# Layer 1's norms in one operation per tile, with weights and shifts moved behind the turn

## What is computed

```python
def layer0(q_feat, kv_feat, ...):
    qn  = layer_norm(q_feat,  g_q,  be_q)     # (x - mu) * rsqrt(var + 1e-5) * gamma + beta
    kvn = layer_norm(kv_feat, g_kv, be_kv)
    q = einsum('bnq,eq->bne', qn,  Wq) + bq
    k = einsum('bmk,ek->bme', kvn, Wk) + bk
    v = einsum('bmk,ek->bme', kvn, Wv) + bv
    attn = softmax(einsum('bne,bme->bnm', q, k))
    return q_feat + einsum('bne,fe->bnf', attn @ v, Wd) + bd

def layer1(x, ctx, mask, ...):                # 8 heads of 256
    Q, K, V = x @ Wq, ctx @ Wk, ctx @ Wv
    attn = softmax(where(mask, Q K^T / 16, -inf))
    return layer_norm((attn @ V) @ Wo + x, gamma, beta)
x = layer0(x, ctx_768, ...)
return layer1(x, ctx_768, mask, ...)
```

## Time and profile before

| | before |
|---|---|
| median of 3 runs | 502.14 us (501.59 to 502.42) |
| the profiled execution: its time | 503.23 us |
| its span, first to last instruction | 501.4 us |
| mean granted TensorE clock | 0.995 |
| TensorE busy in the span | 473.7 us |
| VectorE, ScalarE, POOL busy | 332.4, 290.8, 244.6 us |

### The profile page before, as it was taken

The page is one execution under the profiler, slowest core; times in us unless marked ns, Lnnn a source line. Parts: engine busy times, 40 slices in busy tenths (PEclk is TensorE's granted clock), DMA queues, the critical chain, the costliest instruction groups (busy, mean ns, idle before and its releaser), DMA issues.

```text
span 501.4 us, 7564 instructions
## 1 busy us (share of the span) xinstructions
PE 473.7 (94%) x2424; PEld 395.0 (79%) x2424; DVE 332.4 (66%) x681; ACT 290.8 (58%) x480; POOL 244.6 (49%) x151
## 2 busy tenths in 40 slices
PE   0999999999999999999999999999999999999993
PEld 0777787777878888888888888888888888778893
DVE  4999866476685658565856585667657665664566
ACT  3657477468665656565656565666556564646331
POOL 4636763555855363627172727363635453353003
PEclk9999999999999999999999999999999999999998
DMA  8413004667865656565647474747484746661002
GB/s 261 147 44 126 1 25 123 210 203 231 251 201 187 209 169 209 169 210 167 221 156 230 147 225 156 250 136 254 142 256 135 244 149 190 171 205 43 1 1 84
DMA packets 53974, 81.97 MB, mean 163 GB/s; under 512 B 5792, under 2 KB 43072, under 8 KB 53824
## 3 DMA queue, kind: packets, MB, share of 16 engines
q1 hardware_dynamic: 44992, 50.16, 34.5%
q10 hardware_dynamic: 8960, 31.54, 16.8%
HBM read 49.16 MB, written 32.51 MB: 163 GB/s over the span
## 4 chain that ended last, share of the span: by engine, by line
PE 79%; DVE 8%; ACT 4%; issue 3%; DMA 3%; POOL 2%; SPq 1%; DVEq 0%; POOLq 0%; ACTq 0%
PE ps_scores L621 29%; PE ps_o L645 6%; PE ps_o L653 6%; PE ps_o L646 6%; PE ps_o L652 6%; PE ps_o L647 6%; PE ps_task L569 3%; PE ps_task L568 3%; PE ps_task L567 3%; DMA ctx_raw<-in_context 2%; PE ps_out L567 2%; PE ps_out L568 1%; PE ps_out L569 1%; PE ps_turn L637 1%; PE ps_out L739 1%
## 5 line engine op out<-in xcount | busy, mean ns | idle before, releaser
L514 POOL TENSOR_TENSOR probs_t_lo<-probs_t_lo,probs_t_hi 128x1024 fp32r<-128x1024 f32 (+1 forms) x75 | 146.7, 1968 | 177.2 <-ACT probs_t_hi L1013 177.2
L1013 ACT ACTIVATE probs_t_hi<-probs_t_lo 128x1024 fp32r<-128x1024 f32 (+1 forms) x75 | 64.6, 881 | 38.4 <-DMA probs_t_lo<-scratch 37.9
L621 PE MATMUL ps_scores<-key_hi,q_hi 128*128 128x512 f32 x144 | 57.7, 401 | 1.3 <-DVE neg_scores L1346 0.8
L1333 DVE RECIPROCAL row_inv<-row_sum 128x1 f32<-128x1 f32 x72 | 11.2, 158 | 71.9 <-PE ps_scores L621 70.1
L645 PE MATMUL ps_o<-probs_t_hi,val_hi 128*128 128x512 f32 (+1 forms) x144 | 56.7, 394 | 1.5 <-issue 0.9
L621 PE MATMUL ps_scores<-key_rem,q_lo 128*128 128x512 f32 x144 | 56.6, 393 | 0.5 <-DVE q_lo L1428 0.3
L621 PE MATMUL ps_scores<-key_rem,q_hi 128*128 128x512 f32 x144 | 56.6, 393 | 0.0
L621 PE MATMUL ps_scores<-key_lo,q_hi 128*128 128x512 f32 x144 | 56.6, 393 | 0.0
L621 PE MATMUL ps_scores<-key_hi,q_lo 128*128 128x512 f32 x144 | 56.4, 392 | 0.0
L646 PE MATMUL ps_o<-probs_t_lo,val_hi 128*128 128x512 f32 (+1 forms) x144 | 56.4, 391 | 0.0
L653 PE MATMUL ps_o<-probs_t_lo,val_rem 128*128 128x512 f32 (+1 forms) x144 | 56.3, 392 | 0.0
(11 more groups left out here) (254 smaller groups left out, 1094.4 us busy)
## 6 DMA issues: line engine op xcount, KB each, us to landing
probs_t_lo<-scratch SPq DMA_DIRECT2D x240, 128.0 KB, 3.0
...
```

The source lines that it names most:

```text
L514: nc.gpsimd.tensor_tensor(pt_lo[b][:, t, k, :], pt_lo[b][:, t, k, :].bitcast(f32), moved_part(j, k).bitcast(f32), ALU.subtract).then_inc(m ...
L621: last = pe.matmul(ps_scores[:, n], left, right[:, n], start=(i == 0), stop=(i == len(passes) - 1))
L1013: act.activation(moved_part(j, k), pt_lo[b][:, t, k, :].bitcast(f32), ACT.Copy)\
```

## The change

A layer-0 norm becomes one operation per tile: (x - mean) / sigma. ScalarE does it for x and for half of the context as scale and bias, with the bias (-mean/sigma) made by a new small VectorE operation (`shift_means`, which needs POOL's result); VectorE does it for the other context half with a two-scalar operation (`norm_context`). Gamma is applied later, where the turned chunks leave PSUM: features then lie on partitions, and gamma is a column, given as scale to ScalarE's rounding and to VectorE's subtraction; likewise when B leaves PSUM. The columns come from four 2-row transposes of the norm rows on PE (`gains`). The betas go into biases: VectorE reduces the weights against a broadcast beta row (`fold_bias`), PE adds products with `neg_be` to the query bias (T_VEC). The score shift is made on PE: w = two-part bias product (4 products), the constant (4), and 16 narrow products of the turned x with w in two parts (`turn_shift`), once for each batch. `sum_shift` and POOL's `bias_tiles` go. The context of batch 0 is loaded in two halves, `q_rows` is not broadcast any more, one kv row of 192 values is, behind the first weights; the norm rows come in three small DMAs ahead of the identity on ScalarE's queue. Roundings and waits change places as shown.

```diff
             sp.dma_start(resid[:, 0:QT, :], x_tiles[:, 0:QT, :]).then_inc(x_loaded[0], 16)
-            sp.dma_start(q_rows[:, :, :], rows_q.partition_broadcast(P)).then_inc(q_rows_loaded, 16)
-            sp.dma_start(ctx_raw[:, 0:KT, :], ctx_tiles[:, 0:KT, :]).then_inc(ctx_loaded[0], 16)
-            sp.dma_start(kv_rows[:, :, :], rows_kv.partition_broadcast(P)).then_inc(kv_rows_loaded, 16)
+            sp.dma_start(ctx_raw[:, 0:CTX_HALF, :], ctx_tiles[:, 0:CTX_HALF, :]).then_inc(ctx_loaded[0], 16)
+            sp.dma_start(ctx_raw[:, CTX_HALF:KT, :], ctx_tiles[:, CTX_HALF:KT, :]).then_inc(ctx_loaded[1], 16)
             sp.dma_start(ring[0][:, :], weights_a[0]).then_inc(ring_loaded[0], 16)
+            sp.dma_start(kv_row[:, :], rows_kv[1].partition_broadcast(P)).then_inc(kv_row_loaded, 16)
...
-            def bias_tiles(b, tiles, scaled_before, done):
...
-                done = b * (QT + CTX_HALF)
-                rsqrt(b, KT, LN_TILES, 2 * b + 1)
-                pool.wait_ge(q_rows_loaded, 16)
-                bias_tiles(b, range(KT, LN_TILES), done, x_normed)
+                rsqrt(b, KT, LN_TILES, 3 * b + 1)
...
-                rsqrt(b, 0, KT, 2 * b + 2)
-                pool.wait_ge(kv_rows_loaded, 16)
-                bias_tiles(b, range(CTX_HALF, KT), done + QT, ctx_normed[1])
+                rsqrt(b, 0, CTX_HALF, 3 * b + 2)
+                rsqrt(b, CTX_HALF, KT, 3 * b + 3)
...
-            pool.wait_ge(centred, LN_TILES + QT)
+            pool.wait_ge(x_normed, 2 * QT)
...
+            def turn_shift(b, bank):
+                for t in range(QT):
+                    q = slice(b * QUERIES + t * P, b * QUERIES + (t + 1) * P)
+                    for k in range(DT):
+                        pe.matmul(bank[:, 2 * t:2 * t + 2], xt_hi[:, k, q], w_pair[:, k, :], start=(k == 0), stop=False)
+                        last = pe.matmul(bank[:, 2 * t:2 * t + 2], xt_lo[:, k, q], w_pair[:, k, :],
+                                         start=False, stop=(k == DT - 1))
+                last.then_inc(shift_turned, 1)
...
-            pe.wait_ge(spread_made, DT)
-            pe.wait_ge(ring_loaded[0], 16)
-            raw = ring[0]
-            for k in range(DT):
...
             pe.wait_ge(ident_loaded, 16)
+            pe.wait_ge(norm_rows_loaded, 48)
+            for n in range(N_GAINS):
...
+            last.then_inc(gains_turned, 1)
             for c in range(X_CHUNKS):
                 turn_chunk(0, c)
             pe.wait_ge(piece_split, PC_A0 + 1)
             absorb(T_A0, 0)
             absorb(T_A0b, 1)
-            for n in range(3):
...
             for c in range(X_CHUNKS, CHUNKS):
                 turn_chunk(0, c)
+            pe.wait_ge(bias_folded, 1)
             pe.wait_ge(chunk_split, X_CHUNKS)
-            pe.wait_ge(task_free, T_VEC + 1)
+            raw = ring[0]
+            for d in range(DT):
+                for k in range(DT):
+                    last = pe.matmul(w_bank[:, d:d + 1], raw[:, k * DIM + d * P:k * DIM + (d + 1) * P],
+                                     bias_cols[:, k:k + 1], start=(k == 0), stop=(k == DT - 1))
+            last.then_inc(w_made, 1)
+            pe.wait_ge(task_free, T_A0b + 1)
+            pe.wait_ge(gains_made, 1)
+            for n in range(2):
...
+            last.then_inc(task_done, 1)
+            pe.wait_ge(chunk_split, X_CHUNKS)
             queries(T_Q0, 0, 0)
             queries(T_Q0b, 0, 1)
+            pe.wait_ge(w_split, 1)
+            for n in range(2 * DT):
+                last = pe.matmul(w_bank[:, DT:DT + 1], ones[:, :], shift_parts[:, n:n + 1],
+                                 start=(n == 0), stop=(n == 2 * DT - 1))
+            turn_shift(0, w_bank[:, V_SHIFT:V_SHIFT + 2 * QT])
             pe.wait_ge(chunk_split, CHUNKS)
...
+                if c == 0:
+                    pe.wait_ge(task_free, T_Q1 + 1)
+                    turn_shift(1, ps_task[:, 0:2 * QT])
...
+            act.dma_start(norm_rows[:, 0:DIM], rows_q).then_inc(norm_rows_loaded, 16)
+            act.dma_start(norm_rows[:, DIM:DIM + CTX], rows_kv).then_inc(norm_rows_loaded, 16)
+            act.dma_start(norm_rows[:, DIM + CTX:2 * DIM], rows_kv[:, P:CTX]).then_inc(norm_rows_loaded, 16)
+            act.dma_start(ident[:, :], identity).then_inc(ident_loaded, 16)
             act.dma_start(cols[:, :], vectors).then_inc(cols_loaded, 16)
-            act.dma_start(ident[:, :], identity).then_inc(ident_loaded, 16)
...
-            def scale_tiles(b, tiles, rstds):
...
+            def norm_tokens(b):
+                act.wait_ge(means_made, 2 * b + 1)
+                for t in range(KT, LN_TILES):
+                    n, x_tile = b * LN_TILES + t, b * QT + t - KT
+                    act.activation(xn[:, x_tile, :], resid[:, x_tile, :], ACT.Identity,
+                                   scale=rstd[:, n:n + 1], bias=neg_means[:, n:n + 1]).then_inc(x_normed, 1)
+            def norm_context(b):
+                act.wait_ge(means_made, 2 * b + 2)
...
-            act.wait_ge(cols_loaded, 16)
-            for n in range(2 * DT):
-                act.activation(spread[:, n, :], ones[:, :], ACT.Copy, scale=cols[:, C_BK + n:C_BK + n + 1])\
-                    .then_inc(spread_made, 1)
-            scale_tiles(0, range(KT, LN_TILES), 1)
+            act.activation(row_sum[:, 0:1], ones[:, 0:1], ACT.Copy)
+            norm_tokens(0)
             round_weights(16, 0)
+            act.wait_ge(gains_made, 1)
             for c in range(X_CHUNKS):
                 round_chunk(0, c)
-            scale_tiles(0, range(CTX_HALF, KT), 2)
+            norm_context(0)
+            double_context(0, 0)
             round_a(T_A0, 0, -1.0)
             round_a(T_A0b, 1, -1.0)
-            double_context(0, 0)
-            round_chunk(0, 2)
             double_context(0, 1)
-            for c in range(3, CHUNKS):
+            for c in range(2, CHUNKS):
                 round_chunk(0, c)
-            round_weights(16, 1)
             act.wait_ge(vec_made, 1)
             round_queries(T_Q0, 0, 0, 0)
             round_queries(T_Q0b, 0, 1, 0)
+            round_weights(16, 1)
+            act.wait_ge(bias_folded, 2)
+            for n in range(DT, 2 * DT):
+                act.activation(spread[:, n, :], ones[:, :], ACT.Copy, scale=bias_cols[:, n:n + 1]).then_inc(spread_made, 1)
             exp(-1, 0)
             round_b(T_B0, 0)
             round_b(T_B0b, 1)
             round_probs(-1, 0)
             exp(-1, 1)
-            scale_tiles(1, range(KT, LN_TILES), 3)
+            norm_tokens(1)
             round_weights(32, 0)
             round_probs(-1, 1)
             exp(-1, 2)
...
-            def ln_centre(b, tiles):
...
+            def norm_context(b):
+                dve.wait_ge(rstd_made, 3 * b + 2)
+                for t in range(CTX_HALF):
                     n = b * LN_TILES + t
...
+                    dve.tensor_scalar(kvn[b][:, t, 0:CTX], ctx_raw[:, b * KT + t, :], moments[:, n, 0:1],
+                                      rstd[:, n:n + 1], ALU.subtract, ALU.mult).then_inc(ctx_normed[0], 1)
+            def shift_means(b, first, end, rstds):
+                n = slice(b * LN_TILES + first, b * LN_TILES + end)
+                dve.wait_ge(rstd_made, 3 * b + rstds)
+                dve.scalar_tensor_tensor(neg_means[:, n], moments[:, n, 0], -1.0, rstd[:, n], ALU.mult, ALU.mult)\
+                    .then_inc(means_made, 1)
+            def fold_bias(side, raw, loaded):
+                dve.wait_ge(loaded, 16)
+                for k in range(DT):
+                    n = side * DT + k
+                    first = (DT + k if side == 0 else k) * DIM
+                    dve.tensor_tensor_reduce(
+                        out=probs[:, n * CTX:(n + 1) * CTX], in0=raw[:, first:first + CTX], in1=kv_row[:, :], scale=1.0,
+                        scalar=0.0, op0=ALU.mult, op1=ALU.add, accum_out=bias_parts[:, n:n + 1]).then_inc(bias_summed, 1)
...
+                dve.tensor_tensor(bias_cols[:, n], bias_parts[:, n],
+                                  cols[:, C_BK + side * DT:C_BK + (side + 1) * DT], ALU.add).then_inc(bias_folded, 1)
+            def split_w():
...
+                dve.tensor_tensor(w_pair[:, :, 1], made, w_pair[:, :, 0].bitcast(f32), ALU.subtract).then_inc(w_split, 1)
...
-            def sum_shift(b, tiles):
...
+            def finish_shift(b, bank):
...
-            dve.wait_ge(q_rows_loaded, 16)
-            ln_centre(0, x_token_tiles)
-            ln_stats(0, range(KT), ctx_loaded[0])
-            ln_moments(0, 0, KT)
+            ln_stats(0, range(CTX_HALF), ctx_loaded[0])
+            ln_moments(0, 0, CTX_HALF)
+            shift_means(0, KT, LN_TILES, 1)
+            ln_stats(0, range(CTX_HALF, KT), ctx_loaded[1])
+            ln_moments(0, CTX_HALF, KT)
+            dve.wait_ge(gains_turned, 1)
+            dve.tensor_copy(gains[:, :], vec_bank[:, V_GAINS:V_GAINS + 2 * N_GAINS])
...
             dve.wait_ge(piece_hi, HI_OF[PC_A0])
```

(33 more changed lines are left out.)

169 lines of the change are left out of this document (86 added, 83 removed).

## The result

The changed kernel took 510.84 us (median of four executions, 509.51 to 513.83) against 501.88 us for the kernel before (501.59 to 502.42) beside it: ratio 1.0189, interval 1.017 to 1.0208. The sign of the forecast was right; the size, +2.95 us, was a third of the 8.96 us measured, and the time lies outside the range. The profiled execution took 513.83 us, the longest of the four, its span 512.0.

What follows compares the result with a forecast made beforehand. TensorE, busy 94% of the span, was taken as the bound. Front +0.55, power wait +1.2 and batch 1's shifts +1.2 gave +2.95: profiled 503.23 becomes 506.2, and the median, 1.1 lower, 505.1 us (slower); range 501.2 to 507.0.

Steps and rivals of the forecast that it cites:

- The price of the narrow products: Front, before queries and scores: a one-column f32 product costs 0.12 us; w 4, query biases 12, constant 4 products.
- The clock: TensorE's front: no clock fall was forecast; products were priced at full-clock spacings, such as 0.235 us per query product.
- +0.55 forecast: Front, up to the end of the first scores: 0.55 us later than before, between -1.5 and +1.9.
- Rival C: Front: TensorE's slow start covers the weights' product, 2.9 instead of 1.45 us; with late loads +2.3, 506.9 us; chance 0.14.
- The loads: Front: 459 kB less ahead of the weights, landing at 9.9 to 10.8 instead of 12.0 us; first context half at 7.0.
- The cover for the identity: Front: the identity, moved to fourth on ScalarE's queue and wanted at about 10 us, is hidden by the x norm.
- The shifts: 16 narrow fp32r products at 0.12 us, 1.9 us in the front and among batch 0's values; net there +1.2.
- rival A: Front and values: narrow fp32r products cost 0.06 us each, 0.95 less in both places; +1.05, 503.2 us; chance 0.15.
- The power wait: Between minimum 0 and 1: VectorE's shift_means waits 1.1 us for POOL's power, plus 0.1 for the operation; +1.2 us.
- Rival D: Between minimum 0 and 1: VectorE's wait for POOL's power hides, 1.2 us less, 503.9 us; chance 0.13.
- Hidden work: VectorE before the first minimum: second fold (0.85 us) and small operations end 0.7 us before the scores, costing nothing.
- After 62 us: Rest of the kernel: assumed only to repeat what it did, shifted, its stream keeping its length; no cost.

Runs made afterwards that it cites:

- b1_narrow: Kernel before plus 14 narrow f32 products (28 instructions, results thrown away) in one piece behind its own: 509.98 us, ratio 1.013.
- b2_mixed: Kernel before plus 28 narrow instructions, scattered one or two products at a time between the wide query products: 507.14 us, ratio 1.0087.
- f1: Changed kernel with batch 1's first shift_means moved from ahead of the b splits to behind minimum 1: 510.22 us, ratio 1.0153.
- f3: Changed kernel plus six wide f32 products (results thrown away) on TensorE as soon as x is loaded: 511.68 us, ratio 1.0194.
- f4: Changed kernel with the wide query products ahead of the w and vector products, nothing left out: 510.49 us, ratio 1.0156.
- b3_noshift: Kernel before with the score shift left out and replaced by zero: 501.93 us, ratio 0.9987.
- h1_noshift: Changed kernel with the score shift left out (no w, constant or shift products on TensorE): 504.95 us, ratio 1.0047.
- h2_lean: h1_noshift with the norm's shift folded into the query bias on VectorE, remaining vector products between queries, power subtraction behind minimum 1: 503.63 us, ratio 1.0023.

## Why the prediction was wrong, step by step

*The price of the narrow products: the step that failed first.* The text read "0.95/8" as the price of a product. It is the price of an instruction, and a plain f32 product is two; the row's x8 were four products. So w, the vector and the constant were 8, 24 and 8 instructions where 4, 12 and 4 were priced. From the fold to the first query the sum had 2.0 us; 32 instructions at 0.115 are 3.7. With the constant the miscount is 2.1 us.

*The clock: not in the sum, nor in any rival.* The sum priced every product at the 2.4 GHz level, without a reason given, and this is the largest part of the error. From 21.1 us, inside the vector, the changed kernel's front runs at 1.2 GHz. Worked out from its rows against full speed: 20 narrow instructions at 0.21 instead of 0.115 are 1.9 us, twelve query products (25.25 to 30.51) 5.25 instead of 2.85, the constant 0.3, and in the second fall, in the scores, 1.0. That is 5.6 of the 8.9 us that separate the first minimum's +9.5 from the +0.55 forecast; the miscount is 2.1, and the fold 1.4; the shifts give 0.1 back. The median execution has somewhat less: its mean granted clocks were 0.987 to 0.989, the profiled one 0.981. That the narrow stretch brings such a fall is shown by b1_narrow against b2_mixed, the same number in another place, and by the means: it was 0.990 or less in 19 of 19 executions of the five kernels with 28 or more narrow instructions in one piece (the changed one, b1, f1, f3, f4), and 0.994 or more in 72 of 72 of the kernel before. That nothing else brings one is not so (b3_noshift). Rival C had a slow clock, but at the start of TensorE's work, for lack of work before. That part came true (weight products 2.7 us instead of 1.45, transposes 1.97), is hidden largely by the chain that sets the fold, and f3_warm, which takes it away at a price of its own, gains nothing.

*The loads.* The first half of the context was there by 6.1 and not at 7.0 (a value below the sum's own 7.2 to 8.5); but its other half came at 9.54, the identity at 8.60 and the weights at 11.22, later than the 9.9 to 10.8 of the sum, so the fold ended at 19.6, not at 18.3, and TensorE went on at 19.7. The cover for the identity held: the x transposes waited for ScalarE. TensorE's wait for the fold was 0.8 us, not 1.5, as chunks were turned later too.

*The shifts: right.* 16 fp32r products with two columns took 1.79 us in the front (31.73 to 33.52) and 1.70 at the values, 0.11 each at full clock; 0.12 was priced, and rival A's 0.06 is out. The 25 ns that the prediction quotes from the Trainium skill ("TensorE: Matmul & The Clock Gate", section "Back-to-back issue gap") for a lone product aren't seen here, where each product has its own load row; that the load sets the spacing is likely and not shown. From the values to the fifth minimum's scores the stream was 1.24 us longer, with 1.2 forecast. Ahead of the values came 0.4 that the sum didn't have: TensorE waited 0.87 us for batch 1's lower x part instead of 0.46, so from the fourth to the fifth minimum it is 1.6 longer.

*The power wait: right.* VectorE stood 1.12 us for GpSimd (forecast 1.1), minimum 1 came 5.9 us after minimum 0 (forecast 5.7, before 4.5), so 1.4 stand for the 1.2 of the sum. Rival D is out. f1_power takes 1.1 us of it back.

*Hidden work.* The second fold was costed at nothing behind a lead of 0.7 us, and in the changed kernel it cost nothing, as TensorE was later still. In h1_noshift and h2_lean it was the next thing on the path, through GpSimd: one sum took 2.55 us instead of 0.35, one addition 2.20. "Were that lead gone" was the right condition with the wrong price.

*After 62 us.* The prediction took the stream to keep its length, and said that it would be wrong otherwise. About 1.9 us came back in the changed kernel, and 1.7 were lost in b2_mixed. This stays open, and it is as large as the effect of the last edits. In the profiled execution it makes the error of the sum smaller: 8.9 too little in the front, 0.2 in the power wait, 0.4 at the values, and 1.9 too much here give the 7.6 between +2.95 and +10.6.
